# Graph network on one core: message operands kept in PSUM, column one-hots made by POOL

## The chip, the cores and the metric

The kernel runs on 1 core of one Trainium2 chip. The metric is the device time of one execution in microseconds; less is better. TensorE is called PE here, VectorE DVE, ScalarE ACT, GpSimd POOL and SyncE SP.

## The reference

`x` has 18750 nodes of 64 features, and there are 318750 edges (`src`, `dst`) with one noise value each. After a layer norm and a ReLU, two layers run; each computes a gate for every edge, sums the gates by `src`, and sends weighted features along the edges:

```python
def _denoise_gcn_layer(x, row, col, noise, ...):
    ...
    mask = jnp.clip(gate * (ZETA - GAMMA) + GAMMA, 0.0, 1.0)[:, 0]
    rowsum = jax.ops.segment_sum(mask, row, num_segments=N_NODES) + EPS_DEG
    d_inv_sqrt = jnp.clip(rowsum ** (-0.5), 0.0, 10.0)
    vals = mask * d_inv_sqrt[row] * d_inv_sqrt[col]
    msg = vals[:, None] * f2
    return jax.ops.segment_sum(msg, row, num_segments=N_NODES)
...
x = x + x0 + x1 + x2
```

## The kernel before, in words

The edges are first sorted by row inside groups of 2048. Such a group is a superstep: ST = 2048 edges, as 128 lanes of CT = 16 slots, and T = 156 supersteps hold all edges. Because `dst` is ordered, the column nodes of one superstep lie in a window of 128 nodes. The kernel checks that once and takes the local path (`is_local`); the other path (`Else`) isn't run with these inputs. For each of the two layers L, the stages follow one another: nodes (matmuls with the weights), masks (one superstep at a time), y (the features times d_inv_sqrt, written to HBM as three bf16 parts of each f32, `local_y`), messages, and buckets, in which POOL gathers the messages of each bucket of rows from HBM by indirect DMA and PE sums them.

The change lies in the **message stage**. For superstep t, with h = t % 2 and u = t % 4:

- SP (`load_superstep`, L467 to L474) spreads the 2048 column offsets of the superstep from `crelp_d` in HBM over all 128 partitions of SBUF (`bcast`, two buffers, L471), once the one-hots of t-2 are made; then it loads the window of y, 128 rows of 3 x 64 bf16 (L474), once PE is done with t-2. SP runs its instructions in order.
- DVE (`col_hots`, L1229 to L1233) compares the offsets with the partition's number; the result is a 128 x 2048 one-hot in bf16, in one of two buffers (`col_one_hots`). It waits for the spread and for PE's matmuls of t-2.
- PE (`spread_y`, L1577 to L1587) multiplies each slot's 128 x 128 one-hot by the three parts of the window, adding them up in PSUM: 16 x 3 = 48 matmuls, the result 128 x 1024 f32, two banks of `psG`, two such sets. It waits for the one-hots, for the window, and for the multiply of t-2.
- DVE (`scale`, L1238) multiplies this by the masks `ga` into `scaled` in SBUF (two buffers).
- ACT (`first_bf16`, L805) copies `scaled` as bf16 into `staged`, and L806 puts the rows' lane numbers beside it; DVE (`first_rest`, L1243) subtracts the copy from `scaled`; ACT (`second_bf16`, L810) copies the remainder as bf16; DVE (`last_part`, L1247) subtracts that and writes the third bf16 part.
- ACT (`store_messages`, L814) issues the store of the superstep's 784 KB to `msg_d`.

`messages_local` (L1249) writes out DVE's order: scale(t), last_part(t-1), col_hots(t+2), first_rest(t). ACT's order (`body_local`, L817) is first_bf16(t), the store of t-1, second_bf16(t). POOL has nothing to do in this stage: it waits for the stores and then issues the gathers of the bucket stage (`load_windows`, L580). In the mask stage it runs small operations of 32 elements (`split_masks`, L558 to L565).

`crelp_d` is written once, ahead of the layers: PE transposes the columns, ACT copies them (L661) and, reordered, into `lane_turned` (L663), and SP stores 156 pieces (L390).

Of the kernel before, what the change touches and what calls it, by code (L numbers as in the profile page):

```python
# [5 lines left out]
N, D, E = 18750, 64, 318750  # L6
P = 128
HI = -(-N // P)
NP = P * HI
CH = 8  # L10
# [48 lines left out]
def build(nc, x, src, dst, noise, params, out):  # L59
    f32, bf16, i32, u16, i16 = mybir.dt.float32, mybir.dt.bfloat16, mybir.dt.int32, mybir.dt.uint16, mybir.dt.int16  # L60
# [7 lines left out]
    crelp_d = nc.dram_tensor("crelp_d", (EP,), u16).ap()  # L68
# [12 lines left out]
    with ctx:  # L81
# [110 lines left out]
        lane_turned = turned_a  # L192
# [36 lines left out]
        scaled = flat_merge[:, 0:2 * CT * D].rearrange("p (h j d) -> p h j d", h=2, j=CT)  # L229
# [99 lines left out]
        def _(sp):  # L329
# [90 lines left out]
            for L in range(2):  # L420
# [95 lines left out]
        def _(pool):  # L516
# [26 lines left out]
            for L in range(2):  # L543
# [29 lines left out]

                def load_windows(b):
# [31 lines left out]
                with pool.If(is_local):  # L606
                    for u in range(4):
# [12 lines left out]
        def _(act):  # L620
# [70 lines left out]
            for L in range(2):  # L691
# [109 lines left out]
                def first_bf16(i, u):  # L801
# [3 lines left out]
                    act.activation(staged[:, u, :, 0:D], scaled[:, u % 2, :, :], ACT.Copy).then_inc(first_part, 1)  # L805
                    act.activation(staged[:, u, :, MW:MW + 1].bitcast(u16), row_lane[:, bass.ds(t * CT, CT)].unsqueeze(2), ACT.Copy)  # L806

                def second_bf16(t, u):
                    act.wait_ge(rest_ready, L * T + t + 1)
                    act.activation(staged[:, u, :, D:2 * D], scaled[:, u % 2, :, :], ACT.Copy).then_inc(second_part, 1)  # L810
# [38 lines left out]
        def _(dve):  # L849
# [224 lines left out]
            for L in range(2):  # L1074
# [154 lines left out]
                def col_hots(i, h):  # L1229
                    t = i * 2 + h  # L1230
                    dve.wait_ge(msg_index_loaded[h], (L * T // 2 + i + 1) * 16)
                    wait(dve, y_taken, L * T + t - 1)
                    dve.tensor_scalar(col_one_hots[:, h, :], bcast[:, 2 * h:2 * h + 2, :].rearrange("p a e -> p (a e)"), pid[:, 0:1], None, ALU.is_equal).then_inc(col_hots_ready, 1)  # L1233

                def scale(t, h):
                    dve.wait_ge(y_taken, L * T + t + 1)
                    wait(dve, third_part, L * T + t - 1)
                    dve.tensor_tensor(scaled[:, h, :, :], psG[:, 2 * h:2 * h + 2, :].rearrange("p a (j d) -> p (a j) d", d=D),  # L1238
                                      ga[:, bass.ds(t * CT, CT)].unsqueeze(2).to_broadcast([P, CT, D]), ALU.mult).then_inc(scaled_ready, 1)

                def first_rest(t, u):
                    dve.wait_ge(first_part, L * T + t + 1)
                    dve.tensor_tensor(scaled[:, u % 2, :, :], scaled[:, u % 2, :, :], staged[:, u, :, 0:D], ALU.subtract).then_inc(rest_ready, 1)  # L1243

                def last_part(t, u):
                    dve.wait_ge(second_part, L * T + t + 1)
                    dve.tensor_tensor(staged[:, u, :, 2 * D:MW], scaled[:, u % 2, :, :], staged[:, u, :, D:2 * D], ALU.subtract).then_inc(third_part, 1)  # L1247

                def messages_local(i):  # L1249
                    last = isinstance(i, int) and i == T // 4 - 1  # L1250
                    for u in range(4):
                        t = i * 4 + u
                        scale(t, u % 2)
# [40 lines left out]
                with dve.If(is_local):  # L1294
# [5 lines left out]
                    for h in range(2):  # L1300
                        col_hots(0, h)
# [74 lines left out]
        def _(pe):  # L1376
# [79 lines left out]
            for L in range(2):  # L1456
# [120 lines left out]
                def spread_y(i):  # L1577
                    for h in range(2):
                        t = i * 2 + h
# [58 lines left out]
```

## Time and profile before

| | us |
|---|---|
| median of 3 runs (lowest, highest) | 6455.31 (6450.32, 6471.18) |
| the profiled execution | 6455.86 |
| its span, first to last instruction | 6454.1 |
| busy: DVE, PE, ACT, POOL | 5279.6, 4433.2, 2500.7, 1241.8 |
| message stage, multiplies of layer 0 | 2640.6 to 3282.1 |
| message stage, multiplies of layer 1 | 5042.8 to 5684.3 |
| mean granted clock of PE | 0.682 |

The page gives one profiled execution. A busy share over the whole span mixes stages with different limits, so the views that carry the argument are taken over a stretch of one stage. Idle time before a group of instructions is put down to what ended it. PE's matmuls are pipelined and their ends are modelled, so a burst of them is read by its first start and its length in the order of time.

### The profile page before, as it was taken

Reading aid. Unit: us, or ns where it says so; the run is one execution under the profiler, and the core shown is the slowest. Engines: PE = TensorE matmul, PEld = TensorE weight load, DVE = VectorE, ACT = ScalarE, POOL = GpSimd, SP = SyncE. Lnnn points to the kernel's source line nnn. Section 1 sums busy time; section 2 is a strip of 40 time slices with the busy share of each in tenths; the row PEclk is TensorE's granted clock in tenths of the full one; section 3 lists DMA queues with packets and bytes.
Section 4 is the critical chain, followed back from the end, with each engine's and each line's share of the span. In section 5 each row is a group of like instructions: output and inputs, shape, how many; then the busy total and the mean of one; then the engine's idle time right before and its main releaser. Section 6 shows DMA issues by size and latency. Waiting matters only on the chain. (4 is left out here: it accounts for less than half of the span.)

```text
span 6454.1 us, 166440 instructions
## 1 busy us (share of the span) xinstructions
PE 4433.2 (69%) x58388; PEld 3992.8 (62%) x58388; DVE 5279.6 (82%) x10519; ACT 2500.7 (39%) x5126; POOL 1241.8 (19%) x1562
## 2 busy tenths in 40 slices
PE   3777777775878887355556767978885455557766
PEld 2666666664468887344446666578885354446666
DVE  8999999996459998899976666079998999966666
ACT  2666666662345554355520000445553455510000
POOL 0000000000013333000025444023332000035444
PEclk9777777775555555677778898555555667778888
DMA  2000000000456665799979988066665899979998
GB/s 67 0 0 0 0 0 0 0 0 9 12 190 232 233 234 169 260 333 333 332 245 250 248 245 233 0 216 231 232 233 161 286 332 331 333 232 252 250 251 227
DMA packets 438061, 1160.68 MB, mean 180 GB/s; under 512 B 211241, under 2 KB 216974, under 8 KB 437402
## 3 DMA queue, kind: packets, MB, share of 16 engines
q1 hardware_dynamic: 316671, 549.99, 27.3%
q0 software_dynamic: 75264, 354.33, 20.1%
q10 hardware_dynamic: 46036, 255.30, 10.4%
q8 instruction: 40, 0.66, 0.0%
q14 instruction: 50, 0.41, 0.0%
HBM read 936.26 MB, written 281.94 MB: 189 GB/s over the span
## 5 line engine op out<-in xcount | busy, mean ns | idle before, releaser
L1585 PE MATMUL psG<-y_window,area 128*128 128x64 bf16 x14976 | 678.2, 218 | 769.7 <-DVE area L1233 612.3
L1585 PEld LDWEIGHTS psG<-y_window,area 128*128 128x128 bf16 x14976 | 634.2, 115 | 814.0 <-issue 500.9
L1598 PE MATMUL psG<-work,edge 112*128 112x192 bf16 x7104 | 770.2, 277 | 393.2 <-DVE edge L1268 392.8
L1598 PEld LDWEIGHTS psG<-work,edge 112*128 112x128 bf16 x7104 | 726.7, 150 | 436.0 <-DVE edge L1268 350.2
L580 POOL DMA_INDIRECT work<-msg_d,widx x444 | 543.7, 1225 | 2063.6 <-issue 1633.9
L636 ACT ACTIVATE work<-iota,work 128x149 bf16<-128x149 f32 x2496 | 788.9, 406 | 0.0
L1407 PE MATMUL psG<-area,work 128*128 128x112 bf16 x2496 | 551.3, 390 | 337.7 <-DVE area L965 337.7
L1407 PEld LDWEIGHTS psG<-area,work 128*128 128x128 bf16 x2496 | 357.7, 149 | 486.3 <-issue 342.3
L1400 PE MATMUL psG<-work,merge 128*128 128x148 bf16 x4992 | 544.4, 293 | 69.8 <-ACT work L636 69.8
L1400 PEld LDWEIGHTS psG<-work,merge 128*128 128x128 bf16 x4992 | 527.7, 132 | 92.2 <-issue 66.3
L1268 DVE TENSOR_TENSOR edge<-y_edge,ids 112x2048 bf16<-112x2048 int16 x444 | 524.8, 1223 | 23.1
L810 ACT ACTIVATE work<-merge 128x1024 bf16<-128x1024 f32 x312 | 329.7, 1057 | 549.1 <-DVE merge L1243 549.1
L743 ACT ACTIVATE edge<-merge,npid 128x2048 bf16<-128x2048 uint16 x156 | 312.4, 2003 | 475.6 <-DMA merge<-crel_d 469.4
L805 ACT ACTIVATE work<-merge 128x1024 bf16<-128x1024 f32 x312 | 329.8, 1057 | 197.8 <-issue 93.1
L951 DVE SCALAR_TENSOR_TENSOR work<-merge,work,psG 128x148 bf16<-128x148 f32 x1248 | 367.6, 366 | 39.1 <-ACT work L627 39.1
L951 DVE SCALAR_TENSOR_TENSOR area<-merge,work,psG 128x148 bf16<-128x148 f32 x1248 | 367.6, 366 | 25.1 <-DVE work L946 18.2
L1247 DVE TENSOR_TENSOR work<-merge,work 128x1024 bf16<-128x1024 f32 x312 | 382.4, 1226 | 2.2 <-ACT work L810 2.2
L1238 DVE TENSOR_TENSOR merge<-psG,edge 128x1024 f32<-128x1024 f32 x312 | 380.1, 1218 | 2.6 <-PE psG L1585 2.6
L1243 DVE TENSOR_TENSOR merge<-merge,work 128x1024 f32<-128x1024 f32 x312 | 380.3, 1219 | 1.0 <-ACT work L805 1.0
L1263 DVE TENSOR_TENSOR ids<-work,shift 112x32 int16<-112x32 int16 x222 | 47.4, 214 | 363.4 <-DMA work<-msg_d,widx 363.4
L1598 PE MATMUL psG<-area,merge 112*128 112x192 bf16 x2304 | 250.0, 277 | 108.6 <-DVE merge L1268 108.6
L558 POOL TENSOR_SCALAR area<-area 128x32 f32<-128x32 f32 x156 | 64.1, 411 | 1315.4 <-ACT area L759 1315.4
(254 smaller groups left out, 8330.7 us busy)
## 6 DMA issues: line engine op xcount, KB each, us to landing
msg_d<-work ACTq DMA_DIRECT2D x312, 784.0 KB, 4.6
area<-rlo_d SPq DMA_DIRECT2D x312, 512.0 KB, 4.2
merge<-crel_d SPq DMA_DIRECT2D x312, 512.0 KB, 5.0
area<-crelp_d SPq DMA_DIRECT2D x312, 512.0 KB, 5.7
y_window<-y_d SPq DMA_DIRECT2D x312, 48.0 KB, 3.7
work<-msg_d,widx POOLq DMA_INDIRECT x444, 10.0
y_d<-cur SPq DMA_DIRECT2D x7, 1008.0 KB, 3.8
y_d<-work SPq DMA_DIRECT2D x7, 1008.0 KB, 4.8
```

What stands on the lines that cost most here:

```text
L580: pool.indirect_dma_start(out=windows[par][0:WP, g, :, :].rearrange("p s w -> p (s w)"), out_offset=None, in_=msg_d, in_offset=bass.Indire ...
L636: ins = act.activation(below[:, h, k, :], iota_all[:, :], ACT.Sign, bias=keyf[:, bass.ds(t * CT + k, 1)], scale=-1.0)
L805: act.activation(staged[:, u, :, 0:D], scaled[:, u % 2, :, :], ACT.Copy).then_inc(first_part, 1)
L951: ins = dve.scalar_tensor_tensor(picks[h][:, k, :], iota_half, keyf[:, bass.ds(t * CT + k, 1)], psG[:, h, 0:HB], ALU.is_equal, ALU.mult, a ...
L1238: dve.tensor_tensor(scaled[:, h, :, :], psG[:, 2 * h:2 * h + 2, :].rearrange("p a (j d) -> p (a j) d", d=D), ga[:, bass.ds(t * CT, CT)].un ...
L1243: dve.tensor_tensor(scaled[:, u % 2, :, :], scaled[:, u % 2, :, :], staged[:, u, :, 0:D], ALU.subtract).then_inc(rest_ready, 1)
L1247: dve.tensor_tensor(staged[:, u, :, 2 * D:MW], scaled[:, u % 2, :, :], staged[:, u, :, D:2 * D], ALU.subtract).then_inc(third_part, 1)
L1268: dve.tensor_tensor(q_one_hots[s][0:WP, g, :, :], iota_rows[0:WP, :, :], ids[0:WP, s, g * WIN:(g + 1) * WIN].unsqueeze(1).to_broadcast([WP ...
L1400: ins = pe.matmul(psG[:, h, 0:HB], sides[:, s, :], below[:, h, k, s:s + HB], start=s == 0 and k == 0, stop=s == 1 and k == CT - 1)
L1407: ins = pe.matmul(psG[:, 2 + h, 0:RECS * CT], place[:, h, :, k], spread_rec[:, h, :, :, k], start=k == 0, stop=k == CT - 1)
L1585: ins = pe.matmul(psG[:, 2 * h + k // CH, k % CH * D:(k % CH + 1) * D], col_one_hots[:, h, k * P:(k + 1) * P], y_window[:, h, m * D:(m + 1 ...
L1598: ins = pe.matmul(psG[:, slot_, 0:MW], q_one_hots[slot_][0:WP, g, :, s], windows[slot_][0:WP, g, s, 0:MW], start=g == 0 and s == 0, stop=g ...
```

## The change

`scaled` no longer lies in SBUF. It is four sets of two PSUM banks each (`psG` in three pairs, and `psR`); PE writes a superstep's products into set u, DVE multiplies there in place and subtracts there in place, and ACT reads from there. PE waits for the last part of t-4 before it writes the set again, in place of the multiply of t-2. The column one-hots move from DVE to POOL, in a loop of their own that begins once the first piece of y is ready; the multiply no longer waits for a buffer. The offsets are stored in HBM and spread to SBUF as single bytes, so that a spread is 256 KB. A no-op stands ahead of the one-hots on POOL and ahead of the spread on SP. `lane_turned` is written as bytes by ACT.

```diff
-    crelp_d = nc.dram_tensor("crelp_d", (EP,), u16).ap()
+    crelp_d = nc.dram_tensor("crelp_d", (EP,), u8).ap()
...
-        lane_turned = turned_a
+        lane_turned = flat_merge.bitcast(u8)[:, 0:TB]
...
-        scaled = flat_merge[:, 0:2 * CT * D].rearrange("p (h j d) -> p h j d", h=2, j=CT)
+        scaled = [t.rearrange("p a (j d) -> p (a j) d", d=D) for t in [psG[:, 2 * u:2 * u + 2, :] for u in range(3)] + [psR[:, :, :]]]
+        msg_cols = bcast[:, :, :].rearrange("p a e -> p (a e)").bitcast(u8)[:, 0:2 * ST].rearrange("p (h e) -> p h e", h=2)
...
                         wait(sp, col_hots_ready, L * T + t - 1)
-                        sp.dma_start(bcast[:, 2 * h:2 * h + 2, :].rearrange("p a e -> p (a e)"),
-                                     spread(crelp_d, t)).then_inc(msg_index_loaded[h], 16)
+                        sp.nop(nofuse=True)
+                        sp.dma_start(msg_cols[:, h, :], spread(crelp_d, t)).then_inc(msg_index_loaded[h], 16)
...
+                def col_hots(i):
+                    for h in range(2):
+                        t = i * 2 + h
+                        pool.wait_ge(msg_index_loaded[h], (L * T // 2 + i + 1) * 16)
+                        wait(pool, y_taken, L * T + t - 1)
+                        pool.nop(nofuse=True)
+                        pool.tensor_scalar(col_one_hots[:, h, :], msg_cols[:, h, :], pid[:, 0:1], None, ALU.is_equal).then_inc(col_hots_ready, 1)
...
                 with pool.If(is_local):
+                    pool.wait_ge(y3_ready, L * PIECES + 1)
+                    steps(pool, 0, T // 2, col_hots)
...
-                    act.activation(staged[:, u, :, 0:D], scaled[:, u % 2, :, :], ACT.Copy).then_inc(first_part, 1)
+                    act.activation(staged[:, u, :, 0:D], scaled[u], ACT.Copy).then_inc(first_part, 1)
...
-                def scale(t, h):
+                def scale(t, u):
                     dve.wait_ge(y_taken, L * T + t + 1)
-                    wait(dve, third_part, L * T + t - 1)
-                    dve.tensor_tensor(scaled[:, h, :, :], psG[:, 2 * h:2 * h + 2, :].rearrange("p a (j d) -> p (a j) d", d=D),
-                                      ga[:, bass.ds(t * CT, CT)].unsqueeze(2).to_broadcast([P, CT, D]), ALU.mult).then_inc(scaled_ready, 1)
+                    dve.tensor_tensor(scaled[u], scaled[u], ga[:, bass.ds(t * CT, CT)].unsqueeze(2).to_broadcast([P, CT, D]), ALU.mult).then_inc(scaled_ready, 1)
...
-                    dve.tensor_tensor(scaled[:, u % 2, :, :], scaled[:, u % 2, :, :], staged[:, u, :, 0:D], ALU.subtract).then_inc(rest_ready, 1)
+                    dve.tensor_tensor(scaled[u], scaled[u], staged[:, u, :, 0:D], ALU.subtract).then_inc(rest_ready, 1)
...
-                        if not last or u < 2:
-                            col_hots(i * 2 + u // 2 + 1, u % 2)
...
-                    for h in range(2):
-                        col_hots(0, h)
...
-                    for h in range(2):
-                        t = i * 2 + h
+                    for u in range(4):
+                        t, h = i * 4 + u, u % 2
                         pe.wait_ge(col_hots_ready, L * T + t + 1)
-                        pe.wait_ge(y_window_loaded[h], (L * T // 2 + i + 1) * 16)
-                        wait(pe, scaled_ready, L * T + t - 1)
+                        pe.wait_ge(y_window_loaded[h], (L * T // 2 + i * 2 + u // 2 + 1) * 16)
+                        wait(pe, third_part, L * T + t - 3)
...
-                                ins = pe.matmul(psG[:, 2 * h + k // CH, k % CH * D:(k % CH + 1) * D], col_one_hots[:, h, k * P:(k + 1) * P],
+                                ins = pe.matmul(scaled[u][:, k, :], col_one_hots[:, h, k * P:(k + 1) * P],
```

The second copy of ACT (L810) and the last part (L1247) change their operand in the same way, and the end of PE's loop waits for `third_part` in place of `scaled_ready`.

## Rows read from the trace of the kernel before

**Rows 1.** The page's head: busy us, share of the span, instructions.
```profile
span 6454.1 us, 166440 instructions
...
PE 4433.2 (69%) x58388; PEld 3992.8 (62%) x58388; DVE 5279.6 (82%) x10519; ACT 2500.7 (39%) x5126; POOL 1241.8 (19%) x1562
```

**Rows 2.** Busy time by stretch: message stage of layer 0 (granted clock, DMA share, GB/s).
```profile
2850.00:3050.00 200.00, 105.14 (x2310) 98.24 (x2310) 200.00 (x194) 109.26 (x144) 0.00 (x0) 0.72 0.94 332
```

**Rows 3.** Groups of DVE instructions, 2650 to 3280 us: busy, mean ns, idle before.
```profile
L1247 DVE TENSOR_TENSOR work<-merge,work 128x1024 bf16<-128x1024 f32 x153 | 187.5, 1226 | 0.0
L1243 DVE TENSOR_TENSOR merge<-merge,work 128x1024 f32<-128x1024 f32 x152 | 185.3, 1219 | 0.0
L1238 DVE TENSOR_TENSOR merge<-psG,edge 128x1024 f32<-128x1024 f32 x152 | 185.2, 1218 | 0.0
L1233 DVE TENSOR_SCALAR area<-area,pid 128x2048 bf16<-128x2048 uint16 x152 | 113.6, 747 | 0.0
```

**Rows 4.** Line 1238 in layer 0: duration ns min/median/max, first and last start us.
```profile
L1238 DVE TENSOR_TENSOR merge<-psG,edge x156: 1215/1218/1225, 2640.6 to 3282.1; 128x1024 f32<-128x1024 f32 x156
```

**Rows 5.** Order of time, message stage: start us, us, engine, line.
```profile
2826.64 1.22 DVE L1238 TENSOR_TENSOR merge<-psG,edge 128x1024 f32<-128x1024 f32 x1
2826.76 1.06 ACT L810 ACTIVATE work<-merge 128x1024 bf16<-128x1024 f32 x1 [1.71 <-DVE merge L1243]
2827.85 1.23 DVE L1247 TENSOR_TENSOR work<-merge,work 128x1024 bf16<-128x1024 f32 x1
...
2828.99 0.75 DVE L1233 TENSOR_SCALAR area<-area,pid 128x2048 bf16<-128x2048 uint16 x1
...
2829.66 1.22 DVE L1243 TENSOR_TENSOR merge<-merge,work 128x1024 f32<-128x1024 f32 x1
...
2829.80 1.66 PE L1585 MATMUL psG<-y_window,area 128*128 128x64 bf16 x48 [2.40 <-DVE area L1233]
...
2838.09 2.74 PE L1585 MATMUL psG<-y_window,area 128*128 128x64 bf16 x48 [1.24 <-DVE area L1233]
```

**Rows 6.** Waits of PE, 2650 to 3280 us: total, times, longest.
```profile
PE psG L1585 <- DVE area L1233: 231.7, 124, 2.8
```

**Rows 7.** DMA queues and issues, 5055 to 5680 us (KB each, median us to landing).
```profile
q10 hardware_dynamic: 21679, 120.83, 51.3%
q1 hardware_dynamic: 43342, 86.08, 44.0%
...
area<-crelp_d SPq DMA_DIRECT2D x149, 512.0 KB, 5.7
y_window<-y_d SPq DMA_DIRECT2D x150, 48.0 KB, 3.9
```

**Rows 8.** Order of time, first transfer of layer 0's message stage.
```profile
2633.07 0.34 SPq L471 DMA_DIRECT2D area<-crelp_d  x1
...
2636.98 0.75 DVE L1233 TENSOR_SCALAR area<-area,pid 128x2048 bf16<-128x2048 uint16 x1 [3.69 <-DMA area<-crelp_d]
```

**Rows 9.** Order of time on POOL, first 12 us.
```profile
1.98 0.13 POOL L519 IOTA pid<- 128x1 f32 x1
...
2.50 1.09 POOL L524 MEMSET zero<- 128x1195 f32 x1
...
3.83 0.29 POOL L528 TENSOR_SCALAR_AFFINE_SELECT ident<-ident 128x128 f32<-128x128 f32 x1 [0.16 <-POOL eps L526]
...
7.88 2.28 POOL L535 IOTA y_edge<- 128x2048 int16 x1
```

**Rows 10.** POOL's 32-element cast: DVE idle, and all 156 (ns min/median/max).
```profile
1861.09 0.20 POOL L562 CAST area<-area 128x32 bf16<-128x32 f32 x1
...
L562 POOL CAST area<-area x156: 199/534/538, 1861.1 to 4936.9; 128x32 bf16<-128x32 f32 x156
```

**Rows 11.** Groups over the span: operations that read PSUM.
```profile
L1127 DVE TENSOR_TENSOR edge<-psG,area 128x768 f32<-128x768 f32 x156 | 251.2, 1610 | 0.0
...
L777 ACT ACTIVATE merge<-psG 128x512 f32<-128x512 f32 x8 | 4.7, 596 | 22.9 <-PE psG L1567 22.8
```

More of the change, by code:

```diff
@@ L59, in build @@
 def build(nc, x, src, dst, noise, params, out):
-    f32, bf16, i32, u16, i16 = mybir.dt.float32, mybir.dt.bfloat16, mybir.dt.int32, mybir.dt.uint16, mybir.dt.int16
+    f32, bf16, i32, u16, i16, u8 = mybir.dt.float32, mybir.dt.bfloat16, mybir.dt.int32, mybir.dt.uint16, mybir.dt.int16, mybir.dt.uint8
     ALU, ACT, AX = mybir.AluOpType, mybir.ActivationFunctionType, mybir.AxisListType
@@ L809, in second_bf16 @@
                     act.wait_ge(rest_ready, L * T + t + 1)
-                    act.activation(staged[:, u, :, D:2 * D], scaled[:, u % 2, :, :], ACT.Copy).then_inc(second_part, 1)
+                    act.activation(staged[:, u, :, D:2 * D], scaled[u], ACT.Copy).then_inc(second_part, 1)
                 def store_messages(t, u):
@@ L1227, in local_y @@
                     dve.tensor_tensor(parts[:, :, 2 * D:3 * D], rest, parts[:, :, D:2 * D], ALU.subtract).then_inc(y3_ready, 1)
-                def col_hots(i, h):
-                    t = i * 2 + h
-                    dve.wait_ge(msg_index_loaded[h], (L * T // 2 + i + 1) * 16)
-                    wait(dve, y_taken, L * T + t - 1)
-                    dve.tensor_scalar(col_one_hots[:, h, :], bcast[:, 2 * h:2 * h + 2, :].rearrange("p a e -> p (a e)"), pid[:, 0:1], None, ALU.is_equal).then_inc(col_hots_ready, 1)
@@ L1241, in first_rest @@
                 def first_rest(t, u):
                     dve.wait_ge(first_part, L * T + t + 1)
-                    dve.tensor_tensor(scaled[:, u % 2, :, :], scaled[:, u % 2, :, :], staged[:, u, :, 0:D], ALU.subtract).then_inc(rest_ready, 1)
+                    dve.tensor_tensor(scaled[u], scaled[u], staged[:, u, :, 0:D], ALU.subtract).then_inc(rest_ready, 1)
                 def last_part(t, u):
                     dve.wait_ge(second_part, L * T + t + 1)
-                    dve.tensor_tensor(staged[:, u, :, 2 * D:MW], scaled[:, u % 2, :, :], staged[:, u, :, D:2 * D], ALU.subtract).then_inc(third_part, 1)
+                    dve.tensor_tensor(staged[:, u, :, 2 * D:MW], scaled[u], staged[:, u, :, D:2 * D], ALU.subtract).then_inc(third_part, 1)
@@ L1249, in messages_local @@
                 def messages_local(i):
-                    last = isinstance(i, int) and i == T // 4 - 1
                     for u in range(4):
                         t = i * 4 + u
-                        scale(t, u % 2)
+                        scale(t, u)
                         if u > 0 or not isinstance(i, int) or i > 0:
                             last_part(t - 1, (u - 1) % 4)
-                        if not last or u < 2:
-                            col_hots(i * 2 + u // 2 + 1, u % 2)
@@ L1611, in _ @@
                 with pe.If(is_local):
-                    steps(pe, 0, T // 2, spread_y)
-                    pe.wait_ge(scaled_ready, (L + 1) * T)
+                    steps(pe, 0, T // 4, spread_y)
+                    pe.wait_ge(third_part, (L + 1) * T)
                     steps(pe, 0, HI // SLOTS + 1, sum_buckets)
```

1 line of the change is left out of this document (removed).

## The prediction

> **What bounds the kernel now.** I read the page's head first: over the whole span DVE is busy for 82% and no other engine for more than 69% [rows 1]. That is a mean over stages, so I looked at the message stage alone. A 200 us stretch of it has DVE busy for 200.00 us, with PE at 105, ACT at 109 and POOL at nothing [rows 2]; the DMA engines are busy for 0.94 of it. Four groups of DVE instructions make up that time [rows 3]: the multiply out of PSUM (L1238, 1218 ns), the two subtractions (L1243 1219 ns, L1247 1226 ns) and the column one-hots (L1233, 747 ns). None of them has idle time before it. In one layer the multiply starts 156 times between 2640.6 and 3282.1 us [rows 4], so a superstep lasts 641.5 / 155 = 4.14 us, and both layers together hold 312.
>
> The order of time shows how the 4.14 is made [rows 5]. From start to start DVE spends 1.21 us on L1238, 1.14 on L1247, 0.67 on L1233 and, from the 4.14 what is left up to the next multiply, 1.12 on L1243. The 1.21 is in part a wait: ACT's copy L810 starts at 2826.76, lasts 1.06, and L1247 starts 0.03 later. PE takes 1.66 us for the 48 matmuls of one superstep and 2.74 for those of another, the granted clock being 0.72 in the mean [rows 2], between its levels of 1.2 and 2.4 GHz; either way it rests for over a microsecond. Its long wait is for L1233 [rows 6]: PE is served by DVE, not the other way round.
>
> **The change, part by part.**
>
> *One-hots off DVE.* This removes 312 x 0.67 us from DVE's queue = 209 us. The three instructions left take 4.14 - 0.67 = 3.47 us per superstep. ACT sits between them: the multiply, 1.22, ACT's first copy, 1.06, and two hand-overs of 0.03 make 2.34 us before the remainder can start, and the two DVE instructions ahead of it take 1.21 + 1.14 = 2.35. So ACT just fits, and DVE's floor is 3.47.
>
> *Operands in PSUM.* Reading PSUM costs DVE nothing that the rows show: L1238 reads it and takes 1218 ns, L1243 reads only SBUF and takes 1219 [rows 3]. The Trainium skill (VectorE: DVE Perf Modes, the errata table) gives a PSUM source 120 fixed cycles against 58; the two rows disagree, and by the page the two changed subtractions would cost 0.13 us per superstep, 40 us in all if DVE binds. Writing f32 to PSUM from DVE is in no row. A gain is not excluded, but no row shows one: ACT's copy of 512 elements out of PSUM takes 596 ns [rows 11], more than half of the 1.06 us for 1024 in SBUF, so the low end is zero. The far end is the slowest DVE row that touches PSUM, L1127 with 1610 ns for 768 elements, 2.1 ns each [rows 11], which would make each write 2.2 us. That row also reads and writes with strides, and these do not, so I take zero. Four sets of banks replace two buffers. PE waits for the last part of four supersteps ago instead of the multiply of two ago: the chain of 1.7 to 2.7 (PE), three DVE times of 1.2 and two ACT times of 1.06 is 8.4 us at most, against 4 x 3.47 = 13.9. Free.
>
> *One-hots on POOL.* POOL is idle in this stage, so only the duration counts, and no row has 2048 elements read and compared. Nearest rows [rows 9]: a 2048-element iota takes 2.28 us; a memset of 1195 takes 1.09, with the 0.13 of a one-element iota as the fixed part 0.80 ns per element, so 1.8 us for 2048; a select that reads and compares 128 elements takes 0.29, by the same 0.13 1.3 ns per element, so 2.8 us. I take **2.2 us**, nearest the iota that has this size, and keep 1.8 and 2.8. A hand-over lies on either side, 0.03 us as from ACT to DVE [rows 5] or 0.16 as ahead of that select. POOL's operations also suffer from DVE now: the same 32-element cast takes 0.20 us with DVE idle and 534 ns in the median beside it [rows 10]. In the new stage each DVE instruction has one operand in PSUM. The Trainium skill (SBUF — State Buffer, Who interferes with whom) says that a DVE instruction with at most one SBUF input does not hold up GpSimd; no row shows this pairing. If the 0.33 us stays, the period below grows by 0.17 us and the time by 52 us; I leave it out of the sum and inside the range.
>
> *Bytes instead of 16-bit offsets.* The spread drops from 512 to 256 KB per superstep. Now the stage's two queues use 51.3% and 44.0% of the 16 engines [rows 7]: 2.12 us of each 4.14 for the message store, 1.82 for offsets and y windows. Offsets are 512 of the 560 KB there, so about 1.6 us; halving gives 2.12 + 1.82 - 0.8 = 3.1 us if the time goes with bytes, 3.9 if it goes with packets, whose number stays. The transfer's delay matters as much. It lands 5.7 us after issue under this load [rows 7], and with empty queues the first one lets DVE start 3.9 us after issue [rows 8]. Halving takes off 0.8 us of engine time alone and up to 1.6 where it shares the engines with the store: 5.7 less these is 4.1 to 4.9. I take **4.8 us**, near the upper end, because the engines will be as full as now.
>
> *What is late next.* There are two offset buffers, and SP issues the spread for t only after the one-hots of t-2. So two supersteps last at least landing + POOL + hand-overs = 4.8 + 2.2 + 0.2 = 7.2 us, **3.6 us each**, just above DVE's 3.47. At both low ends this loop gives 4.1 + 1.8 + 0.2 = 6.1, 3.1 each, and DVE's 3.47 decides; at both high ends 4.9 + 2.8 + 0.2 = 7.9, 3.95 each. SP's queue also holds the y window behind a wait for PE, two supersteps back: 3.9 (landing) + 2.7 (PE) + 0.2 = 6.8, 3.4 each, just under the others. POOL's own wait, for PE of t-2, gives (2.2 + 2.7 + 0.2) / 2 = 2.6. Nothing else is queued on POOL here; its gathers come after the stage.
>
> *The small edits.* The no-ops on SP and POOL and the bounds of the loops cost nothing against waits of microseconds. ACT's byte-wide copy in the column stage and the byte stores of crelp_d keep their counts. The first one-hots of each layer take 2.2 instead of 0.75 us: +3 us for two layers. The mask, node and bucket stages are untouched.
>
> **Sum.** 312 x (4.14 - 3.60) = 168 us less, 3 us more. The profiled execution took 6455.9 us (its span 6454.1), the median of the three runs 6455.3, so they stand together: 6455.9 - 168 + 3 = **6291 us**. The measurement of this kernel can tell about 0.3% (19 us) from no change.
>
> **Rivals.**
>
> 1. *POOL is the pace, and the kernel is slower.* The 32-element cast with DVE idle takes 0.20 us [rows 10]; against the one-element 0.13 [rows 9] that is 0.07 us for 31 more elements, 2.3 ns each, and 4.8 us for 2048. The offset loop is then 4.8 + 4.8 + 0.2, 4.9 each, and POOL's own queue 4.95: 312 x 0.8 = 253 us more, **6709 us**. It decides from a POOL time of 3.3 us on, where (4.8 + 3.3 + 0.2) / 2 passes 4.14. Against it speak the 128-element select and the iotas; the cast's extra may be fixed cost of reading. 0.12. The Trainium skill (GPSIMD Engine Reference, Performance versus the Vector engine) has about 2.6 cycles per element for two inputs, 4497 ns at 2048, and calls one input roughly line-rate: the first would be this rival, the second my forecast.
> 2. *PSUM writes are slow on DVE*, at the 2.2 us of the far end: 1.14 + 2.2 + 2.2 = 5.5 us per superstep, some 430 us more, 6880 us. 0.03.
> 3. *The transfer lands no sooner.* Packets stay as many and the store still fills the engines: 5.7 + 2.2 + 0.2 = 8.1, 4.05 each, 28 us less, **6431 us**. 0.06.
> 4. *No gain at all*: the DMA engines, 0.94 busy, already set 3.9 to 4.1 us with the same number of packets; about **6450 us**. 0.04. Against it: DVE has no idle time today.
>
> **How the numbers follow.** The forecast, a period from 3.47 to 3.9 us, has 0.75; its own range is 6250 to 6384. Faster takes it and rival 3, 0.81; within 0.3% is rival 4, 0.04; slower takes rivals 1 and 2, 0.15. The range from 6235 to 6435 takes in DVE's floor, with 15 us for a faster PSUM, and reaches up to rival 3, leaving out rivals 1, 2 and 4.
>
> **What would show it.** The multiply starts every 3.5 to 3.7 us; DVE has small idle times before it, ended by PE, and PE's by POOL. The one-hot row on POOL reads about 2.2 us; the subtractions stay near 1.22; the spread is 256 KB and lands in under 5 us; POOL waits on the spread. With POOL at over 3.3 us, or DVE's rows at 1.3 and above, or a landing still at 5.7, the forecast is wrong at that step. If DVE is busy without a gap at 3.47, the loop was priced too high and the time is near 6250.

## The result, and the profile after

The changed kernel takes 6873.92 us in the median of four runs (6858.56 to 6881.23), the kernel before 6456.56 beside it (6450.32 to 6471.18): ratio 1.0625, 95% interval 1.06 to 1.0649. The forecast was 6291 us with a range up to 6435, so it has the wrong sign. The profiled execution took 6876.02 us, its span 6874.2.

First the same 200 us of layer 0's message stage as in [rows 2], in the view by stretch (PE, PEld, DVE, ACT, POOL busy, then granted clock, DMA share and GB/s):

```profile
2850.00:3050.00 200.00, 95.58 (x1776) 89.84 (x1776) 131.41 (x111) 81.66 (x111) 200.00 (x38) 0.56 0.59 206
```

DVE was full and is now at 131 of 200; POOL was empty and is full; the DMA share fell from 0.94 to 0.59. The groups of that stretch (busy, mean ns, idle before and what ended it) name the instruction:

```profile
L581 POOL TENSOR_SCALAR area<-area,pid 128x2048 bf16<-128x2048 uint8 x38 | 205.7, 5430 | 0.0
L1583 PE MATMUL psG<-y_window,area 128*128 128x64 bf16 x1344 | 74.1, 238 | 80.3 <-POOL area L581 57.3 <-DVE work L1250 23.0
L1242 DVE TENSOR_TENSOR psG<-psG,edge 128x1024 f32<-128x1024 f32 x28 | 34.5, 1232 | 54.2 <-PE psG L1583 54.2
L1250 DVE TENSOR_TENSOR work<-psG,work 128x1024 bf16<-128x1024 f32 x28 | 34.0, 1214 | 0.0
L1246 DVE TENSOR_TENSOR psG<-psG,work 128x1024 f32<-128x1024 f32 x27 | 33.3, 1233 | 0.4
```

Each row has its answer in [rows 3, 6]. POOL's one-hots take 5430 ns with no idle time before them; PE waits for them, DVE waits for PE. DVE's three operations, all with an operand in PSUM now, stay at 1214 to 1233 ns. The landing times (2650 to 3450 us; KB each, median us), against [rows 7]:

```profile
area<-crelp_d SPq DMA_DIRECT2D x148, 256.0 KB, 4.3
y_window<-y_d SPq DMA_DIRECT2D x147, 48.0 KB, 1.8
```

One-hots and multiplies of both layers give the pace (duration ns min/median/max, first and last start):

```profile
L581 POOL TENSOR_SCALAR area<-area,pid x156: 5428/5432/5447, 2628.2 to 3468.0; 128x2048 bf16<-128x2048 uint8 x156
...
L1242 DVE TENSOR_TENSOR psG<-psG,edge x117: 1231/1232/1233, 2636.6 to 3469.7; 128x1024 f32<-128x1024 f32 x117
L1242 DVE TENSOR_TENSOR psR<-psR,edge x39: 1232/1233/1233, 2652.7 to 3476.3; 128x1024 f32<-128x1024 f32 x39
...
L1242 DVE TENSOR_TENSOR psG<-psG,edge x117: 1231/1233/1233, 5265.9 to 6100.3; 128x1024 f32<-128x1024 f32 x117
L1242 DVE TENSOR_TENSOR psR<-psR,edge x39: 1231/1233/1233, 5282.1 to 6106.2; 128x1024 f32<-128x1024 f32 x39
```

POOL starts every (3468.0 - 2628.2) / 155 = 5.42 us, its own duration, and so do the multiplies: 839.7 and 840.3 us for the 155 steps of a layer, where they took 641.5 in each before. These two stages hold 198.2 + 198.8 = 397.0 of the 420.1 us that the span grew. Another 28.9 lie between the last multiply of layer 0 and the first of layer 1 (5265.9 - 3476.3 = 1789.6, before 1760.7), and 5.8 come back ahead of and behind them.

### The profile page after: what moved, and what is told of

Same layout as the page of the kernel before. It is cut to its first block and busy times, and to the rows that moved or that the text cites. A ratio compares the mean times of both kernels' runs of the same rounds, so it can differ in the third digit from the quotient of the medians.

```text
span 6874.2 us, 166853 instructions
## 1 busy us (share of the span) xinstructions
PE 4582.1 (67%) x58388; PEld 4133.7 (60%) x58388; DVE 5097.3 (74%) x10207; ACT 2473.8 (36%) x5126; POOL 2930.6 (43%) x1874
## 3 DMA queue, kind: packets, MB, share of 16 engines
q1 hardware_dynamic: 316671, 467.88, 22.9%
## 5 line engine op out<-in xcount | busy, mean ns | idle before, releaser
L581 POOL TENSOR_SCALAR area<-area,pid 128x2048 bf16<-128x2048 uint8 x312 | 1688.6, 5433 | 185.1 <-DMA area<-crelp_d 185.1
L1583 PE MATMUL psG<-y_window,area 128*128 128x64 bf16 x11232 | 593.5, 233 | 854.5 <-POOL area L581 636.4
L1583 PEld LDWEIGHTS psG<-y_window,area 128*128 128x128 bf16 x11232 | 557.4, 125 | 890.6 <-DVE work L1250 561.2
L1596 PE MATMUL psG<-work,edge 112*128 112x192 bf16 x7104 | 788.8, 282 | 366.1 <-DVE edge L1268 365.4
L1596 PEld LDWEIGHTS psG<-work,edge 112*128 112x128 bf16 x7104 | 745.0, 151 | 410.4 <-DVE edge L1268 331.2
L1242 DVE TENSOR_TENSOR psG<-psG,edge 128x1024 f32<-128x1024 f32 x234 | 288.4, 1233 | 461.2 <-PE psG L1583 461.2
L816 ACT ACTIVATE work<-psG 128x1024 bf16<-128x1024 f32 x234 | 239.4, 1023 | 669.6 <-DVE psG L1242 571.3
L1583 PE MATMUL psR<-y_window,area 128*128 128x64 bf16 x3744 | 195.9, 232 | 215.0 <-POOL area L581 145.4
L821 ACT ACTIVATE work<-psG 128x1024 bf16<-128x1024 f32 x234 | 239.4, 1023 | 266.2 <-DVE psG L1246 266.2
```

The source lines that it names most:

```text
L581: pool.tensor_scalar(col_one_hots[:, h, :], msg_cols[:, h, :], pid[:, 0:1], None, ALU.is_equal).then_inc(col_hots_ready, 1)
L816: act.activation(staged[:, u, :, 0:D], scaled[u], ACT.Copy).then_inc(first_part, 1)
L1242: dve.tensor_tensor(scaled[u], scaled[u], ga[:, bass.ds(t * CT, CT)].unsqueeze(2).to_broadcast([P, CT, D]), ALU.mult).then_inc(scaled_read ...
L1583: ins = pe.matmul(scaled[u][:, k, :], col_one_hots[:, h, k * P:(k + 1) * P], y_window[:, h, m * D:(m + 1) * D], start=m == 0, stop=m == 2)
L1596: ins = pe.matmul(psG[:, slot_, 0:MW], q_one_hots[slot_][0:WP, g, :, s], windows[slot_][0:WP, g, s, 0:MW], start=g == 0 and s == 0, stop=g ...
```

## The experiments

Every kernel below is the changed kernel but for the edit shown; where a ratio stands, it is to the kernel before, run beside it. In the four kernels with a shortened comparison (5, 6, 7 and 9) POOL makes the one-hots of only some slots, and the messages of the other slots aren't computed (DVE clears their one-hots once per layer); all other work stays, PE's 48 matmuls per superstep too. Kernels 3, 4, 6 and 7 have one run each and no interval; what is read from them is durations and periods in their traces, and where their time is used it is said to be of one run. A period is the time from one multiply to the next, as above.

**1. One-hots back on DVE, bytes and PSUM sets kept**

```diff
-                    steps(pool, 0, T // 2, col_hots)
...
+                    last = isinstance(i, int) and i == T // 4 - 1
...
+                        if not last or u < 2:
+                            col_hots(i * 2 + u // 2 + 1, u % 2)
```

> The changed kernel with one part undone: DVE makes the column one-hots again, from the bytes, while products and remainders stay in the four sets of PSUM banks. Theory (POOL's one-hot of 5.43 us is the whole loss): the time falls back to DVE's pace. If DVE reads bytes as fast as it read 16-bit offsets (747 ns), a superstep takes 3.47 + 0.67 = 4.14 us, less up to 0.04 by ACT's faster copy, and the kernel 6440 to 6460 us. If DVE is slower on bytes, at one element per cycle of some 1.04 ns (as in its 1024-element rows, 2.3 us in all), a superstep takes 5.6 us and the kernel some 6910; at half that, 1.2 us, 4.6 us and 6600. Rival (PSUM operands slow the stage by themselves): over 4.3 us per superstep even where the one-hot row reads 747 ns.

6622.62 us (before 6469.09), ratio 1.0242, interval 1.0204 to 1.028. DVE's groups, 2700 to 3200 us:

```profile
L1242 DVE TENSOR_SCALAR area<-area,pid 128x2048 bf16<-128x2048 uint8 x107 | 136.8, 1279 | 0.0
L1250 DVE TENSOR_TENSOR psG<-psG,work 128x1024 f32<-128x1024 f32 x81 | 99.5, 1228 | 0.0
```

DVE is the bound again, at (3350.5 - 2632.1) / 155 = 4.63 us per superstep, 0.49 over before. The same comparison takes 1279 ns from bytes and 747 from 16 bits [rows 3], and the 0.53 us between them accounts for it. So bytes suit the transfer and not DVE. The changed kernel, at 1.0625, is nearly 4% slower than even this one. The two losses don't add up to one: in the changed kernel DVE reads no bytes.

**2. The PSUM sets alone** (one-hots on DVE, from 16 bits; the edit is against the kernel before)

```diff
...
-        scaled = flat_merge[:, 0:2 * CT * D].rearrange("p (h j d) -> p h j d", h=2, j=CT)
+        scaled = [t.rearrange("p a (j d) -> p (a j) d", d=D) for t in [psG[:, 2 * u:2 * u + 2, :] for u in range(3)] + [psR[:, :, :]]]
...
-                        wait(pe, scaled_ready, L * T + t - 1)
+                        wait(pe, third_part, L * T + t - 3)
...
```

> Only the PSUM part of the change: four sets of banks, DVE makes the one-hots from 16-bit offsets as before. Theory (POOL is the whole loss, PSUM is free): the multiply starts every 4.10 to 4.15 us and the kernel takes 6435 to 6465 us, ratio to before 0.997 to 1.002. Rival (writing PSUM costs DVE, or PE's wait for the last part of t-4 holds it): 4.25 us and more per superstep, 6490 us and more.

6467.64 us against 6469.09, ratio 0.9999, interval 0.998 to 1.0018. DVE's groups over the same stretch:

```profile
L1250 DVE TENSOR_TENSOR psG<-psG,work 128x1024 f32<-128x1024 f32 x91 | 111.6, 1226 | 0.0
L1254 DVE TENSOR_TENSOR work<-psG,work 128x1024 bf16<-128x1024 f32 x91 | 111.5, 1225 | 0.0
L1246 DVE TENSOR_TENSOR psG<-psG,edge 128x1024 f32<-128x1024 f32 x91 | 111.4, 1224 | 0.0
L1242 DVE TENSOR_SCALAR area<-area,pid 128x2048 bf16<-128x2048 uint16 x121 | 90.0, 744 | 0.0
```

Nothing is gained or lost. The errata table that the prediction weighed (the Trainium skill, VectorE: DVE Perf Modes) has 62 cycles more for a PSUM source; the prediction's estimate from it, 0.13 us per superstep for the two subtractions, would have shown as 40 us with DVE full, ratio 1.006, and the interval excludes it. So the PSUM sets aren't the loss.

**3. POOL's one-hots with DVE's operands in SBUF again** (one run; PE writes two PSUM buffers again)

```diff
...
+        scaled = [flat_merge[:, (u % 2) * CT * D:(u % 2 + 1) * CT * D].rearrange("p (j d) -> p j d", d=D) for u in range(4)]
...
-                    dve.tensor_tensor(scaled[u], scaled[u], ga[:, bass.ds(t * CT, CT)].unsqueeze(2).to_broadcast([P, CT, D]), ALU.mult).then_inc(scaled_ready, 1)
+                    wait(dve, third_part, L * T + t - 1)
+                    dve.tensor_tensor(scaled[u], products[u % 2], ga[:, bass.ds(t * CT, CT)].unsqueeze(2).to_broadcast([P, CT, D]), ALU.mult).then_inc(scaled_ready, 1)
...
-                        wait(pe, third_part, L * T + t - 3)
+                        wait(pe, scaled_ready, L * T + t - 1)
...
```

> The changed kernel with scaled back in two SBUF buffers: POOL makes the one-hots from bytes while DVE's two subtractions read two SBUF operands each. Theory A (POOL's 5.43 us is its own per-element loop, DVE does not matter): the POOL row stays at 5.4 us and the kernel at 6870 us. Theory B (DVE holds POOL up through SBUF, also in the changed kernel in part): the POOL row grows by the time of the DVE instructions with two SBUF operands, 0.5 to 2.4 us, and the kernel takes 7030 us or more.

7053.36 us. The groups, 2700 to 3200 us:

```profile
L582 POOL TENSOR_SCALAR area<-area,pid 128x2048 bf16<-128x2048 uint8 x84 | 506.7, 6049 | 0.0
...
L1252 DVE TENSOR_TENSOR work<-merge,work 128x1024 bf16<-128x1024 f32 x83 | 120.5, 1452 | 0.0
L1244 DVE TENSOR_TENSOR merge<-psG,edge 128x1024 f32<-128x1024 f32 x83 | 101.6, 1225 | 185.9 <-PE psG L1585 185.9
```

With both operands of the subtractions in SBUF the same POOL instruction takes 6049 ns, 0.62 more, and DVE's last part 1452, 0.23 more. Over 312 supersteps POOL's 0.62 is 193 us, near the 177 by which the times of the two profiled executions differ. So the PSUM part earns something only once POOL works: with it POOL keeps 5430 ns in the message stage. The section that the prediction cited (the Trainium skill, SBUF — State Buffer, Who interferes with whom) has it that a DVE instruction with at most one SBUF input doesn't contend with POOL and one with two does; the trace agrees, with POOL at 5430 ns beside the former and 6049 beside the latter. It also calls the contention an exclusive lock, by which the later would wait for the other's end, and here the trace differs: the last part is held in 145 of 312 supersteps, up to 2651 ns, and each held one ends 0.65 us ahead of the end of POOL's instruction. At its usual 1.22 us it has then run within POOL's last 1.9 us.

**4. POOL's price by itself.** Nine operations on POOL at the start of the kernel, each waiting for the one before, and the same nine later (one run):

```diff
...
+                        ins = pool.tensor_scalar(o, src_, pid[:, 0:1], None, ALU.is_equal)
...
+                        ins = pool.tensor_copy(o, src_)
...
```

> The changed kernel with nine POOL operations added twice ahead of the layers, each waited for: compare from 2048 bytes, 2048 16-bit integers, 2048 bf16, 1024 bytes, 1024 f32, then on 2048 bf16 a compare with a constant, a multiply and a copy, and a copy of 2048 bytes. The first set runs after 12 us, when DVE has nothing to do but wait for the input; the second beside DVE's sorting. Theory A (POOL's own loop): the first set's compare from 2048 bytes takes 5.2 to 5.5 us, that from 1024 about 2.8, so about 2.6 ns per element with little fixed time, and the type changes it by less than a tenth. Theory B (DVE stretches it): 2.2 to 3 us in the first set and more in the second. Theory C (bytes are slow to read): bf16 or f32 take 3 us or less where bytes take 5.4.

6898.45 us. POOL in order of time (start, duration):

```profile
11.86 5.46 POOL L552 TENSOR_SCALAR probe<-zero,pid 128x2048 bf16<-128x2048 uint8 x1
17.48 8.45 POOL L552 TENSOR_SCALAR probe<-zero,pid 128x2048 bf16<-128x2048 uint16 x1 [0.17 <-POOL probe L552]
26.10 5.43 POOL L552 TENSOR_SCALAR probe<-zero,pid 128x2048 bf16<-128x2048 bf16 x1 [0.17 <-POOL probe L552]
31.70 2.84 POOL L552 TENSOR_SCALAR probe<-zero,pid 128x1024 bf16<-128x1024 uint8 x1 [0.17 <-POOL probe L552]
34.70 2.84 POOL L552 TENSOR_SCALAR probe<-zero,pid 128x1024 bf16<-128x1024 f32 x1 [0.17 <-POOL probe L552]
37.71 5.36 POOL L554 TENSOR_SCALAR probe<-zero 128x2048 bf16<-128x2048 bf16 x1 [0.16 <-POOL probe L552]
43.24 5.45 POOL L556 TENSOR_SCALAR probe<-zero,pid 128x2048 bf16<-128x2048 bf16 x1 [0.17 <-POOL probe L554]
48.83 1.89 POOL L558 COPY probe<-zero 128x2048 bf16<-128x2048 bf16 x1
50.85 1.89 POOL L558 CAST probe<-zero 128x2048 bf16<-128x2048 uint8 x1
```

The message stage's 5430 is what the operation costs away from that stage too: 5.46 from bytes, 5.43 from bf16, 5.36 against a constant, 5.45 as a product, 2.84 for 1024 elements whether bytes or f32. A copy or cast of 2048 takes 1.89. So a comparison or product with a scalar costs about 2.5 ns per element whatever the type, nearly three times a copy. With that the type of the offsets costs POOL nothing, DVE's PSUM operands cost nothing (kernel 2), and what the changed kernel loses in its message stages is POOL's price alone. Neither of the figures cited for rival 1 from the Trainium skill (GPSIMD Engine Reference: 4497 ns in Performance versus the Vector engine, "roughly line-rate" in Engine selection) fits this form: a scalar operand doesn't make it a one-input operation at line rate, and the 4497 ns for two inputs is 17% short of 5430. The measurement decides. The 8.45 isn't the price of 16 bits: the same operation takes 5.43 in the later set. In that time DVE runs two casts with both sides in SBUF:

```profile
17.29 1.76 DVE L913 CAST work<-work 104x3072 f32<-104x3072 int32 x1
18.96 1.75 DVE L915 CAST work<-work 104x3072 f32<-104x3072 int32 x1
```

They last 3.4 us together, and POOL's instruction, begun 0.2 us after the first of them, is 3.0 longer.

**5 and 6. A cheaper comparison: 768 and 1280 of the 2048 columns** (6 and 10 of the 16 slots; the edit is that of 768)

```diff
...
-                        pool.tensor_scalar(col_one_hots[:, h, :], msg_cols[:, h, :], pid[:, 0:1], None, ALU.is_equal).then_inc(col_hots_ready, 1)
+                        pool.tensor_scalar(col_one_hots[:, h, 0:768], msg_cols[:, h, 0:768], pid[:, 0:1], None, ALU.is_equal).then_inc(col_hots_ready, 1)
...
+                    dve.memset(scratch[:, 0:ST], 0.0)
...
```

> The changed kernel, but POOL compares only the first 768 of each 2048 columns; the rest of the one-hots is zero, so 10 of 16 slots get no message. By the measured 0.25 us and 2.53 ns per element POOL then takes 2.2 us, the value that the prediction took, and everything else of the change stands. If the price of POOL was the only wrong step, the multiply starts every 3.47 to 3.6 us and the kernel takes 6250 to 6295 us, ratio 0.966 to 0.975. Since the spread lands after 4.3 us in the changed kernel, the offset loop gives (4.3 + 2.2 + 0.2) / 2 = 3.35 and DVE's 3.47 should decide: near 6252. Rival (a second limit was missed: PE, the y window, the DMA engines): 3.8 us and more, over 6350 us.

> As the run with 768 columns, with 1280 (6 of 16 slots get no message): POOL takes 0.25 + 1280 x 2.53 ns = 3.49 us. Theory (two offset buffers make a loop of landing and POOL): (4.3 + 3.5 + 0.2) / 2 = 4.0 us per superstep, kernel near 6415 us. Rival (POOL's own pace alone counts, the loop has slack): 3.5 to 3.6 us, kernel 6260 to 6290 us.

768 columns: 6377.52 us (before 6473.51), ratio 0.9853, interval 0.9826 to 0.9879. 1280 columns, one run: 6505.57. POOL's group in each, 2700 to 3200 us:

```profile
L581 POOL TENSOR_SCALAR area<-area,pid 128x768 bf16<-128x768 uint8 x130 | 286.2, 2203 | 216.7 <-DMA area<-crelp_d 197.8 <-PE psG L1584 14.1 <-PE psR L1584 4.8
```

```profile
L581 POOL TENSOR_SCALAR area<-area,pid 128x1280 bf16<-128x1280 uint8 x120 | 421.7, 3517 | 83.6 <-DMA area<-crelp_d 82.9 <-issue 0.2
```

The periods from the first and last multiply are (3232.3 - 2636.0) / 155 = 3.85 and (3288.5 - 2635.5) / 155 = 4.21 us. Both are over what was expected (3.47 to 3.6, and 4.0). With POOL at 2203 ns, the very price the prediction took, the kernel is faster than before: that price alone turned the sign. From 2203, 3517 and 5430 ns the rate is (5430 - 2203) / 1280 = 2.52 ns per element and the fixed part 0.27 us. But 3.85 isn't the 3.6 that the prediction gave for this price. A second step is wrong too, by about 0.25 us. In the order of time of the 768 kernel (SP's issues, PE's bursts, POOL):

```profile
2916.04 4.38 POOL L581 TENSOR_SCALAR area<-area,pid 128x768 bf16<-128x768 uint8 x2 [3.59 <-DMA area<-crelp_d]
...
2918.37 1.57 PE L1584 MATMUL psG<-y_window,area 128*128 128x64 bf16 x48 [1.90 <-POOL area L581]
...
2921.28 0.33 SPq L475 DMA_DIRECT2D y_window<-y_d  x1
...
2922.20 0.34 SPq L473 DMA_DIRECT2D area<-crelp_d  x1
```

PE's burst ends at 2919.94, yet SP issues the y window only at 2921.28, 1.34 later, and the next spread 0.92 after that. The one-hots that free the spread's buffer were done at 2920.42. The spread is issued 1.78 us after them, where 0.21 is enough when SP is free (kernel 9): it stands about 1.6 us in SP's queue, behind a window that waits for PE.

**7. 768 columns with offsets of 16 bits** (one run)

```diff
...
-    crelp_d = nc.dram_tensor("crelp_d", (EP,), u8).ap()
+    crelp_d = nc.dram_tensor("crelp_d", (EP,), u16).ap()
...
```

> As the run with 768 columns, but the offsets stay 16-bit, so a spread is 512 KB (10 of 16 slots get no message). Theory (bytes buy the shorter period): the stage's DMA time of 3.9 us and the loop (5.8 + 2.2 + 0.2) / 2 = 4.1 hold it at 3.95 to 4.1 us, kernel 6395 to 6445 us. Rival (the spread's size does not matter once DVE is relieved): 3.5 us as with bytes, kernel 6255 us.

6586.08 us. POOL stays at 2201 ns, the spread of 512 KB lands in 5.8 us in place of 4.3, and the period is (3330.4 - 2639.6) / 155 = 4.46, over both the expected 3.95 to 4.1 and its rival. Beside kernel 5 the bytes are worth 0.6 us per superstep, some 200 us: without them the move to POOL would be a loss even at 2.2 us. This is what rival 3 asked; it would have had 4.05 for this case. That SP's queue, missing there as well, makes up the rest is likely and not shown.

**8. Shared one-hots: POOL those of even supersteps, DVE those of odd ones.** POOL reads bytes, DVE 16 bits; there are four buffers of offsets and four of one-hots, and spreads are issued two supersteps ahead.

```diff
...
+                        if u < 2:
+                            spread_cols(i, u + 2)
+                        elif not isinstance(i, int) or i < T // 4 - 1:
+                            spread_cols(i + 1, u - 2)
...
+                        if u == 1:
+                            odd_hots(i, 3)
+                        elif u == 3 and (not isinstance(i, int) or i < T // 4 - 1):
+                            odd_hots(i + 1, 1)
...
```

> A version meant to beat both: POOL makes the one-hots of even supersteps from bytes, DVE those of odd ones from 16-bit offsets; four buffers each for offsets and one-hots, each spread issued two supersteps ahead, PSUM sets as in the changed kernel. POOL needs 5.43 us per two supersteps, DVE 3.47 + 0.67 / 2 = 3.80 us each, the DMA engines about 3.5. Theory: 3.80 to 3.85 us per superstep, about 10 us more for the second set of column copies ahead of the layers, kernel 6355 to 6385 us, ratio 0.984 to 0.989. Rival (DVE's one-hot reads SBUF in its fast form and is held up by POOL's 5.43 us, or holds it up): the DVE row for the one-hots grows from 744 ns to over 2 us, and the kernel is no faster than before, 6450 us or more.

6434.79 us (before 6473.51), ratio 0.9952, interval 0.9933 to 0.9971: faster than both kernels, by 0.5% over the one before. The period is (3257.6 - 2647.5) / 155 = 3.94, where 3.80 to 3.85 was expected. DVE's one-hots of layer 0 (ns min/median/max) say why it isn't more:

```profile
L1261 DVE TENSOR_SCALAR area<-area,pid x39: 743/1151/4801, 2639.9 to 3244.7; 128x2048 bf16<-128x2048 uint16 x39
L1261 DVE TENSOR_SCALAR merge<-area,pid x39: 743/748/2659, 2653.3 to 3252.4; 128x2048 bf16<-128x2048 uint16 x39
```

The instruction that took 744 ns in kernel 2 now takes up to 4801, close to the length of one instruction on POOL. In the order of time:

```profile
2876.78 5.43 POOL L597 TENSOR_SCALAR merge<-area,pid 128x2048 bf16<-128x2048 uint8 x1 [2.69 <-DMA area<-crelb_d]
2881.46 1.30 DVE L1261 TENSOR_SCALAR area<-area,pid 128x2048 bf16<-128x2048 uint16 x1
2884.87 5.43 POOL L597 TENSOR_SCALAR area<-area,pid 128x2048 bf16<-128x2048 uint8 x1 [2.66 <-DMA area<-crelb_d]
2889.66 1.19 DVE L1261 TENSOR_SCALAR merge<-area,pid 128x2048 bf16<-128x2048 uint16 x1
```

POOL ends at 2882.21 and 2890.30, and DVE's one-hot, already begun, ends at 2882.76 and 2890.85, both times 0.55 us later. It is held until POOL's instruction is over, whatever is left of that: of the 156 one-hots on DVE, the 100 that take over 780 ns all end 0.54 or 0.55 us after the POOL instruction in which they began. The rule of the section cited at kernel 3 (the Trainium skill, SBUF — State Buffer, Who interferes with whom), that whichever of DVE in a 2-port mode and POOL issues first blocks the other fully, fits, if DVE's one-hot runs in such a mode, which no trace shows.

**9. 768 columns, the spread issued ahead of the y window's wait**

```diff
...
+                        if h == 0:
+                            spread_cols(i, 1)
+                        elif not isinstance(i, int) or i < T // 2 - 1:
+                            spread_cols(i + 1, 0)
...
```

> The 768 column kernel again (POOL makes 6 of the 16 one-hots; messages of the other ten slots are left out), with one edit: SP issues the spread of superstep t+1 ahead of the y window of t, so that the spread is no longer queued behind the window's wait for TensorE. Theory (SP's order sets the period: in the 768 run each loop over three supersteps holds two issues of SP of about 1 us each, one behind the other): the period falls from 3.86 to 3.47 to 3.6 us, VectorE's three PSUM operations become the bound, some 6250 to 6295 us, ratio 0.966 to 0.973. Rival (landing times or TensorE's burst set the 3.86): unchanged, about 6375 us, ratio 0.985.

6348.14 us (before 6467.61), ratio 0.9815, interval 0.9784 to 0.9847. The result lies between the theories: the period fell from 3.85 to (3209.1 - 2634.4) / 155 = 3.71. Its order of time shows two loops:

```profile
2892.41 0.34 SPq L472 DMA_DIRECT2D area<-crelp_d  x1
...
2897.37 2.20 POOL L589 TENSOR_SCALAR area<-area,pid 128x768 bf16<-128x768 uint8 x1 [1.65 <-DMA area<-crelp_d]
...
2897.80 0.33 SPq L482 DMA_DIRECT2D y_window<-y_d  x1
...
2899.78 0.34 SPq L472 DMA_DIRECT2D area<-crelp_d  x1
...
2901.41 2.74 PE L1592 MATMUL psG<-y_window,area 128*128 128x64 bf16 x48 [1.99 <-DMA y_window<-y_d]
...
2905.40 0.33 SPq L482 DMA_DIRECT2D y_window<-y_d  x1
```

Offsets: issue 2892.41, POOL from 2897.37 to 2899.57, next issue into that buffer 2899.78, so 7.37 us for two supersteps, 3.69 each. Window: issue 2897.80, PE from 2901.41 to 2904.15, next issue into that buffer 2905.40, 7.60 for two, 3.80 each. Neither has a rest in it, and over the whole layer both must come to the period, so the pair doesn't say which sets the pace. SP's order was one part of the miss, 0.14 us or less (PE's granted clock over 2700 to 3200 us was 0.80 here and 0.73 in kernel 5, and its bursts were shorter). The other is in the window's loop: 1.25 us pass between PE's last matmul and SP's issue. SP isn't waiting then. Once PE is done it loads the window's address from a table (ns min/median/max, 2700 to 3200 us):

```profile
L415 SPq TENSOR_LOAD <-bases x135: 268/842/1452, 2700.3 to 3198.3; - x135
```

Before the issue at 2905.40 this load takes 0.68 us.

**10. The split with POOL's comparison in four instructions of 512 columns**

```diff
...
+                        for c in range(4):
+                            ins = pool.tensor_scalar(hot_sets[u][:, c * ST // 4:(c + 1) * ST // 4], msg_cols[u][:, c * ST // 4:(c + 1) * ST // 4], pid[:, 0:1], None, ALU.is_equal)
...
```

> The split kernel (POOL makes the one-hots of even supersteps, VectorE those of odd ones) with POOL's in four instructions of 512 columns in place of one of 2048. Theory (VectorE's one-hot, which stood up to 4.9 us in the split run, waits for the rest of POOL's running instruction): its longest falls to 2.3 us or less, the mean towards 800 ns, the period from 3.92 to about 3.85 us, some 6410 us, ratio 0.991. Rival (the two engines share something all the time that both run, whatever the length of an instruction): mean stays at 930 to 1090 ns, 6435 us, ratio 0.995. POOL's own work is four times 0.25 + 512 x 2.53 ns = 6.2 us in two supersteps of 3.9, so it is not the pace.

6410.1 us (before 6467.61), ratio 0.991, interval 0.988 to 0.994, the lowest of the complete kernels; its interval and that of kernel 8 overlap a little. The period is (3256.9 - 2651.0) / 155 = 3.91, against 3.94 in kernel 8 and 3.85 expected. The rows that answer to those of kernel 8, with POOL's:

```profile
L1263 DVE TENSOR_SCALAR area<-area,pid x39: 742/974/1265, 2642.4 to 3244.1; 128x2048 bf16<-128x2048 uint16 x39
L1263 DVE TENSOR_SCALAR merge<-area,pid x39: 742/823/1309, 2656.8 to 3251.7; 128x2048 bf16<-128x2048 uint16 x39
...
L598 POOL TENSOR_SCALAR area<-area,pid x156: 1558/1564/2112, 2641.0 to 3235.2; 128x512 bf16<-128x512 uint8 x156
```

The longest one-hot fell from 4801 to 1309 ns, under the length of one piece. POOL's longest, 2112, is 0.55 us over its median: each of the 139 pieces that take over 1.62 us overlaps one of DVE's one-hots, so now POOL is held up too. The medians, 823 and 974, remain above 744, and the mean over 2700 to 3200 us fell only from 1008 to 929 ns, at the edge of what the rival expected, so most of what the two engines cost each other is still there. The operation reads and writes SBUF on DVE, and the three with an operand in PSUM show nothing of the kind (means of 1217 to 1225 ns in both kernels).

## Why the prediction was wrong, step by step

*What bounds the kernel now*: right. DVE was full, and kernel 2, which leaves its work as it was, keeps the time.

*One-hots off DVE*: the saving was real and unused. With POOL's comparison short, DVE is no longer full: 454 of 500 us busy at a period of 3.85.

*Operands in PSUM*: taken as free, and free (kernel 2, 1224 to 1226 ns). The far end of 2.2 us per write didn't occur.

***One-hots on POOL*: this step failed.** It took 2.2 us and kept 1.8 to 2.8; the operation takes 5.43. The estimate leaned on iotas and memsets, which read nothing, and on a 128-element select, and took the number from the row with the right size instead of the right kind. Measured by length the comparison is 2.52 ns per element and 0.27 us fixed. Rival 1 named the mechanism, and its turning point of 3.3 us fits: at 2203 ns the period is 3.85 and at 3517 it is 4.21, just over 4.14. Its 6709 us was short because 5.43 is over 4.8: 312 x (5.42 - 4.14) = 399 of the 420 us. But that rival 1's price came near was luck. It took 2.3 ns per element from a cast of 32 elements, and kernel 4 has a cast of 2048 at 1.89 us, 0.8 ns for each of the elements between: the cast's extra was fixed cost, as the prediction suspected. The trace of before does hold the same instruction on POOL (L558, a minimum with a constant in the mask stage; ns min/median/max), and the prediction passed it over:

```profile
L558 POOL TENSOR_SCALAR area<-area x156: 398/407/819, 1859.6 to 4935.5; 128x32 f32<-128x32 f32 x156
```

Its fastest, 0.40 us, is twice the cast's fastest, 0.20 [rows 10], a sign that this form costs more than a cast. With 32 elements it is mostly fixed cost, so it gives no slope. No row of before had the price; the honest bounds were far wider than 1.8 to 2.8, and a case of its own deserved more than 0.12.

*POOL beside DVE*: left out of the sum, rightly: 5432 ns in the stage against 5.46 and 5.43 at the start. Kernel 3 gives what it would have cost with the old operands, 0.62 us.

*Bytes*: 4.3 us to land in the changed kernel and 4.8 in kernel 9, where the DMA share, 0.88, is near the 0.94 of before; 4.8 was taken. Rival 3 (no sooner) is out: kernel 7 has 5.8.

*What is late next*: the offset loop was right in its parts; kernel 9 runs it at 3.69 us for 3.6. Two things were missing. SP's queue was treated as two loops side by side, where a spread also stands behind the window ahead of it (kernels 5 and 9: up to 0.14 us per superstep). And 0.2 us was put for the hand-over from PE to SP's window issue, where 1.25 to 1.34 pass, with the load of the address in them; in the prediction's own terms the window's loop is then (3.9 + 2.7 + 1.25) / 2 = 3.93 us and not the 3.4 that seemed safe, and with the 3.4 us that the window takes to land in kernel 9 it is 3.7, as long as the offset loop. This doesn't touch the sign, but by it 6291 us could not be had even at 2.2 us: kernel 5 took 6378.

*The DMA engines at 0.94 as the bound* (rival 4): not so. They are at 0.59 in the changed kernel and at 0.84 to 0.91 in kernels 5, 8, 9 and 10.

**Open**: the 28.9 us between the two message stages. Kernels 1 and 2, which don't use POOL in them, have 9.0 and 11.1 there, kernel 9 has 22.9; but kernel 3 uses POOL as the changed kernel does and has 10.8, so POOL's work alone isn't the reason. A part may be no more than spread: the stage of buckets behind layer 1 differs by 16 us over these kernels (761.6 to 777.9 from the last multiply to the end). No run isolates it. Nor was it tried to load the window's address ahead of the wait for PE.

## What to carry to other kernels

Price an instruction on another engine by rows of the same instruction at two lengths; a row of the right size that only writes says nothing, and one short row is mostly fixed cost and gives no slope. Here two comparisons at the start of the kernel would have shown it. Moving work off a full engine pays as long as the receiver's whole time per step is under what is left: POOL's whole one-hot was 56% over that (5.42 to 3.47), and every second one, in short pieces, brought 0.9%. In a loop through a DMA, count the issuing engine's time between wait and issue, an address load above all, and everything queued ahead on it.

## What the runs showed of the hardware that was not expected

- POOL's comparison of a tile with a scalar takes 2.52 ns per element plus 0.27 us (768 to 2048 elements); with uint8, uint16, bf16 and f32 inputs, with a constant and as a product it is within 2% of that (2201 against 2203 ns, 2.84 and 2.84, 5.36 to 5.46 us); a copy or cast of 2048 takes 1.89 us.
- DVE's comparison of 2048 elements takes 744 ns from uint16 and 1279 from uint8.
- A DVE comparison of 744 ns with both sides in SBUF is held until a running POOL instruction ends: up to 4801 ns beside one of 5434, and 1309 at most beside pieces of 1564. The other way, two DVE casts of 3.4 us together went with one POOL instruction of 8.45 us in place of 5.43.
- A DVE subtraction with both inputs in SBUF was held up to 2651 ns beside POOL's comparison, but ended 0.65 us ahead of POOL's end, 145 times of 312; POOL's own mean rose from 5430 to 6049 ns.
- SP issued a transfer 1.25 and 1.34 us after the end of the PE burst it waited for, and another one right behind it 0.92 us later. The load of a transfer's address took 268 to 1452 ns of SP's time, 842 in the median of kernel 9.
